# Stick-breaking attention on eight cores: where two pairs of matmuls stand in TensorE's order within a key block

## Chip, cores and metric

The kernel runs on the 8 cores of one Trainium2 chip, each core on its own one of eight sequences, with no exchange between them. The metric is the device time of the slowest core in microseconds, lower is better.

## What is computed

One transformer layer: a layer norm, then attention and a mixture of experts side by side on the normed input, both added to it.

```python
z = einsum('bhid,bhjd->bhij', q, k) / sqrt(64)      # 32 heads of 64, 2048 tokens
mask = tril(ones((l, l)), k=-1)
lom = where(mask, -softplus(z), 0)
s = flip(cumsum(flip(lom, -1), -1), -1) - lom        # sum over the later keys below the query
att = where(mask, exp(log_sigmoid(z) + s), 0)
o = einsum('bhij,bhjd->bhid', att, v)
x = x + (o @ Wo.T) + moe(xn)                         # 32 experts, top 4, low-rank factors, one shared
```

The cumulative sum runs over keys from the last to the first, so key blocks are worked from the diagonal back to key 0 and carry a running sum.

## The kernel before

A small scheduler (`Sched`) records instructions for each engine in the order in which the Python code calls `Sc.op`. That order is each engine's program order, and nothing reorders it later. Waits follow from what an instruction reads and writes: an instruction waits for the last writer of what it reads and for the readers of what it overwrites.

The stages of a core, in time: layer norm and transposes, small projections and the router, attention (from about 829 to 4870 us of the profiled execution), the output projection with `Wo`, and the experts (from about 5.4 ms on).

Attention handles 16 head pairs. For one head pair (`gen_headpair`) the loop runs over 4 query tiles `qt` of 512 queries, and in each over key blocks `jb` of 128 keys, from `4*qt+3` down to 0: 4, 8, 12 and 16 blocks, 40 in all. The first four blocks of a query tile lie on the diagonal: with `c0` = 384, 256, 128 and 0 they work on 128, 256, 384 and 512 query columns for each head, and the mask is added by a further matmul (line 555). The others ("full blocks") have 512 columns and no mask. For each block and both heads of the pair (`hs` = 0, 1):

- scores: `emit_z` writes k times q into the PSUM pair `zpair[jb % 2]` (line 548). There are two such pairs, so scores of block jb-1 overwrite the pair of block jb+1, and have to wait until ScalarE has read that for `att`. The two heads' matmuls stand on different rows of the array, and the trace shows full blocks' pair as one line "x2".
- ScalarE: `texp` = exp(z) (L606, or L614 for each head where c0 > 0), `sp` = ln(1 + texp) (L609 or L618).
- sum: for each head TensorE adds `tri` times sp (L632) and the running sum `lsb` through a one-row matmul (L638) to the scores in PSUM, and forms the block's column sum in `pbL` (L644). VectorE adds that to `lsb` (L649). As there is one `pbL` for both heads, the second head's L644 waits for the first head's L649.
- ScalarE: `att` = exp of the result (L565 or L571).
- output: att times v adds to `pboA` and `pboB` (L579). At the end of a query tile VectorE copies both to `oF` (L658).

The loop is pipelined by hand. `pend` is the block before (jb+1), whose `att` and output are still to come. In the loop body of block jb the order in which instructions are recorded before the change is: texp and sp of jb; `yield`; att and output of jb+1 (`emit_att_o`), scores of jb-1; `yield`; the six sum matmuls of jb with the VectorE adds; `yield`.

At every second `yield` the caller takes one step of `gen_qkv` for the next head pair: 3 steps that issue 16 weight loads each on GpSimd's queue, 12 steps of 16 matmuls of 128x128 by 512 into `pbq` (L510, "projection units" below, followed by a VectorE copy, L516 or L520), and 8 steps with two transposes each (L526, L529). The generator is used up after 48 of the head pair's 124 yields: the projection units lie in query tiles 0 and 1 (yields 8 to 30), the transposes in the end of tile 1 and the start of tile 2 (yields 32 to 46). The rest of tile 2 and all of tile 3 have neither, nor has any tile of the last head pair. At every third yield one of 112 casts of later weights from DRAM to DRAM is issued, also on GpSimd's queue, until they are used up in the third head pair.

Of the kernel before, what the change touches and what calls it, by code (L numbers as in the profile page):

```python
# [204 lines left out]
def build_program(upto="full", taps=()):  # L205
# [13 lines left out]
    def res(name):  # L219
        if name not in R_:  # L220
            R_[name] = Res(name)
        return R_[name]
# [312 lines left out]
    def gen_headpair(hp):  # L535
# [21 lines left out]
                    start=False, stop=True, skip_group_check=True),  # L557
                    reads=[res("idb"), res("mneg")], writes=[pr[pz]])

        def emit_att_o(pjb, qt, jbmax):  # L560
            zp = pjb % 2
            c0 = 128 * max(pjb - 4 * qt, 0)
            first = (pjb == jbmax)
            if c0 == 0:
                Sc.op("ACT", lambda sc, zp=zp: sc.activation(  # L565
                    t_att[zp][:], zpair_ap[zp][:], AF.Exp),
                    reads=[pr[(0 if zp == 0 else 6)], pr[(0 if zp == 0 else 6) + 1]],
                    writes=[res(f"att{zp}")])
            else:
                for hs in range(2):  # L570
                    Sc.op("ACT", lambda sc, zp=zp, hs=hs, c0=c0: sc.activation(  # L571
                        t_att[zp][:, 512 * hs + c0:512 * hs + 512],
                        zpair_ap[zp][:, 512 * hs + c0:512 * hs + 512], AF.Exp),
                        reads=[pr[(0 if zp == 0 else 6) + hs]], writes=[res(f"att{zp}")])
            oc0 = 0 if first else c0
            for hs in range(2):
                po = PO_BANK[hs]
                p0 = 64 * hs
                Sc.op("PE", lambda t, zp=zp, pjb=pjb, p0=p0, oc0=oc0, first=first, po=po, hs=hs: t.matmul(  # L579
                    pbank[po][0:64, oc0:QT],  # L580
                    t_vtok[:, pjb * 128 + p0: pjb * 128 + p0 + 64],
                    t_att[zp][:, 512 * hs + oc0:512 * hs + 512],
                    start=first, stop=True, skip_group_check=not first),
                    reads=[rvtok, res(f"att{zp}")], writes=[pr[po]])

        for qt in range(NQT):
            jbmax = 4 * qt + 3
# [11 lines left out]
            pend = None  # L599
            for jb in range(jbmax, -1, -1):  # L600
                zp = jb % 2
                zres = zpair_res[zp]
                Dd = jb - 4 * qt
                c0 = 128 * max(Dd, 0)
# [16 lines left out]
                            reads=[res(f"texp{zp}")], writes=[res(f"sp{zp}")])  # L621
                yield
                if pend is not None:
                    emit_att_o(pend, qt, jbmax)
                if jb > 0:
                    emit_z(jb - 1, qt, 0)
                    emit_z(jb - 1, qt, 1)
                yield
                for hs in range(2):
                    pz = (0 if zp == 0 else 6) + hs  # L630
                    h0 = 512 * hs
                    Sc.op("PE", lambda t, zp=zp, h0=h0, c0=c0, pz=pz: t.matmul(  # L632
                        zpair_ap[zp][:, h0 + c0:h0 + QT], t_tri[:],
                        t_sp[zp][:, h0 + c0:h0 + QT],
                        start=False, stop=True, skip_group_check=True),
                        reads=[res("tri"), res(f"sp{zp}")], writes=[pr[pz]])
                    if jb != jbmax:
                        Sc.op("PE", lambda t, zp=zp, h0=h0, c0=c0, pz=pz, hs=hs: t.matmul(  # L638
                            zpair_ap[zp][:, h0 + c0:h0 + QT], t_ones1[:],
                            t_lsb[hs][:, c0:QT],  # L640
                            start=False, stop=True, skip_group_check=True),
                            reads=[res("ones1"), res(f"lsb{hs}")], writes=[pr[pz]])
                    if jb != 0:
                        Sc.op("PE", lambda t, zp=zp, h0=h0, c0=c0: t.matmul(  # L644
                            pbank[2][0:1, c0:QT], t_negones[:],
                            t_sp[zp][:, h0 + c0:h0 + QT],
                            start=True, stop=True),
                            reads=[res("negones"), res(f"sp{zp}")], writes=[pr[2]])
                        Sc.op("DVE", lambda v, hs=hs, c0=c0: v.tensor_tensor(  # L649
                            t_lsb[hs][:, c0:QT], t_lsb[hs][:, c0:QT], pbank[2][0:1, c0:QT], op=ALU.add),  # L650
                            reads=[pr[2], res(f"lsb{hs}")], writes=[res(f"lsb{hs}")])
                yield
                pend = jb
            emit_att_o(pend, qt, jbmax)
            for hs in range(2):
                po = PO_BANK[hs]
                p0 = 64 * hs
# [315 lines left out]
```

How the kernel before makes its waits and increments, by code:

```python
                def body(e, ops=ops):  # L151
                    for waits, fn, inc_key, inc_n in ops:
                        for (s, v) in waits:
                            e.wait_ge(handles[s], v)
                        if fn is not None:
                            inst = fn(e)
                            if inc_n:
                                inst.then_inc(handles[inc_key], inc_n)
```

## Time and profile before

| | us |
|---|---|
| median of 3 runs | 8427.57 (8363.21 to 8457.3) |
| the profiled execution | 8471.23 |
| its span, slowest core (core 6) | 8469.7 |
| spans of the other cores | 8333.5 to 8442.5 |

| engine, core 6 | busy, share of the span |
|---|---|
| TensorE matmul | 71% |
| ScalarE | 34% |
| VectorE | 32% |
| GpSimd | 10% |

The mean granted TensorE clock of the cores is 0.711 to 0.726 of full speed. The page's chain that ended last gives TensorE 49% of the span, DMA 17%, VectorE 11% and ScalarE 10%. A share over the whole span is a mean over stages with different limits; the change touches the attention stage alone, so that is where the rows below are from. In the timelines a matmul's duration runs past the start of the next one, because they are pipelined; the spacing of starts is what a matmul costs in a row of them. All rows are of core 6.

### The profile page before, as it was taken

What the parts mean: (1) busy time and instruction counts of PE and PEld (TensorE: products, weight loads), DVE (VectorE), ACT (ScalarE), POOL (GpSimd) and SP (SyncE); (2) the same over time, 40 slices, a digit from 0 to 9 for tenths busy, and PEclk for the clock granted to TensorE, in tenths of its full rate; (3) what the DMA queues carried; (4) which work ended last, traced back from release to release, by engine and by line L of the source; (5) the groups of instructions that cost most, each with busy time, mean ns of one, the idle gap of its engine ahead of it and who ended that gap; (6) DMA issues with size and microseconds to landing.
All of it is one profiled execution on the core that took longest, in us unless ns stands there. A gap on an engine that the chain in (4) does not pass through costs nothing.

```text
span 8469.7 us, 79587 instructions; the slowest of 8 cores (8333.5 to 8469.7 us)
## 1 busy us (share of the span) xinstructions
PE 5973.4 (71%) x18740; PEld 1687.8 (20%) x18740; DVE 2682.5 (32%) x4660; ACT 2880.7 (34%) x4306; POOL 854.0 (10%) x1617
## 2 busy tenths in 40 slices
PE   2223667788888888888888856377767757766775
PEld 0011211122222222222222122122212121122212
DVE  7211212222222222222222201166146416523550
ACT  0000334344444444444444500154034305412440
POOL 0101120111000111100000010100110010011001
PEclk9866665666665566666656579688877788777788
DMA  2001646510000000000000034211421151133115
GB/s 76 12 4 11 74 51 76 66 12 7 7 6 6 7 8 8 8 6 6 6 6 1 1 86 95 67 52 55 142 92 47 57 173 51 62 100 119 55 39 171
DMA packets 222099, 408.71 MB, mean 48 GB/s; under 512 B 141576, under 2 KB 144032, under 8 KB 215760
## 3 DMA queue, kind: packets, MB, share of 16 engines
q0 software_dynamic: 200592, 353.00, 19.5%
q1 hardware_dynamic: 20784, 50.47, 2.4%
q8 instruction: 171, 2.80, 0.1%
q14 instruction: 280, 2.29, 0.1%
q10 hardware_dynamic: 272, 0.14, 0.0%
HBM read 451.83 MB, written 85.07 MB: 63 GB/s over the span
## 4 chain that ended last, share of the span: by engine, by line
PE 49%; DMA 17%; DVE 11%; ACT 10%; issue 9%; another core or an unknown queue 2%; DVEq 1%; ACTq 0%; SPq 0%; POOL 0%; POOLq 0%
PE pbq L510 7%; PE zp L632 6%; PE zp L638 6%; DMA cd<-scr_cd 5%; ACT att L565 4%; DMA xp<-x 4%; PE pboA L579 4%; PE zp L548 3%; DVE gu L825 3%; PE pbL L644 3%; PE pboB L579 2%; ACT g L817 2%; PE pbL L814 2%; PE zp L814 2%
## 5 line engine op out<-in xcount | busy, mean ns | idle before, releaser
L649 DVE TENSOR_TENSOR lsb<-lsb,pbL 1x512 bf16<-1x512 bf16 (+3 forms) x1152 | 673.5, 585 | 1820.5 <-PE pbL L644 1803.9
L606 ACT ACTIVATE texp<-zp 128x1024 bf16<-128x1024 f32 x448 | 458.3, 1023 | 984.7 <-PE zp L548 789.5
L632 PE MATMUL zp<-sp,tri 128*128 128x512 bf16 (+3 forms) x1280 | 652.0, 509 | 5.9 <-ACT sp L618 5.9
L565 ACT ACTIVATE att<-zp 128x1024 bf16<-128x1024 f32 x448 | 458.0, 1022 | 575.5 <-PE zp L638 569.8
L638 PE MATMUL zp<-lsb,ones 1*128 1x512 bf16 (+2 forms) x1152 | 610.7, 530 | 0.0
L579 PE MATMUL pboA<-att,vtok 128*64 128x512 bf16 (+2 forms) x640 | 347.0, 542 | 372.5 <-ACT att L565 303.2
L644 PE MATMUL pbL<-sp,negones 128*1 128x512 bf16 (+3 forms) x1152 | 559.4, 486 | 66.7 <-DVE lsb L649 66.1
L825 DVE TENSOR_TENSOR gu<-g,pbL 128x512 bf16<-128x512 bf16 x704 | 484.1, 688 | 201.7 <-PE pboB L811 87.3
L797 ACT ACTIVATE zg<-zp 128x512 bf16<-128x512 f32 x64 | 38.2, 597 | 1482.3 <-PE zp L794 1482.3
L825 DVE TENSOR_TENSOR gu<-g,zp 128x512 bf16<-128x512 bf16 x704 | 484.1, 688 | 176.8 <-PE zp L811 64.7
L817 ACT ACTIVATE g<-zp 128x512 bf16<-128x512 f32 x704 | 420.3, 597 | 291.4 <-PE zp L811 233.3
L817 ACT ACTIVATE g<-pboB 128x512 bf16<-128x512 f32 x704 | 420.3, 597 | 242.9 <-PE pboB L811 179.4
L609 ACT ACTIVATE sp<-texp 128x1024 bf16<-128x1024 bf16 x448 | 473.1, 1056 | 41.8 <-ACT texp L606 0.8
L927 PE MATMUL zp<-cd,zd 128*128 128x512 bf16 x1024 | 305.6, 389 | 230.9 <-DMA cd<-scr_cd 225.9
L548 PE MATMUL zp<-q,k 64*128 64x512 bf16 (+3 forms) x1280 | 433.1, 509 | 0.0
L722 PE MATMUL zp<-wo,oF 128*128 128x512 bf16 x1024 | 269.0, 423 | 188.7 <-DVE op L735 141.0
L579 PE MATMUL pboB<-att,vtok 128*64 128x512 bf16 (+2 forms) x640 | 357.1, 558 | 0.0
L614 ACT ACTIVATE texp<-zp 128x128 bf16<-128x128 f32 (+2 forms) x384 | 146.4, 381 | 616.5 <-PE zp L555 598.7
L497 POOL DMA_DIRECT2D wq<-WqT x256 | 135.2, 528 | 2116.2 <-PE zp L555 1071.8
L814 PE MATMUL pbL<-zu,cgu 128*128 128x512 bf16 x704 | 309.9, 440 | 53.2 <-DVE gu L825 46.8
L814 PE MATMUL zp<-zu,cgu 128*128 128x512 bf16 x704 | 304.5, 433 | 57.6 <-DVE gu L825 52.2
L811 PE MATMUL zp<-zg,cgu 128*128 128x512 bf16 x704 | 316.1, 449 | 0.8 <-ACT g L817 0.8
(187 smaller groups left out, 7007.0 us busy)
## 6 DMA issues: line engine op xcount, KB each, us to landing
cd<-scr_cd POOLq DMA_DIRECT2D x256, 512.0 KB, 4.7
cgu<-scr_cgu POOLq DMA_DIRECT2D x136, 704.0 KB, 4.5
scr_cgu<-CguT POOLq DMA_DIRECT2D x32, 704.0 KB, 74.3
x<-x SPq DMA_DIRECT2D x16, 1024.0 KB, 4.9
scr_cd<-CdT POOLq DMA_DIRECT2D x32, 512.0 KB, 72.9
xp<-x SPq DMA_DIRECT2D x64, 256.0 KB, 5.2
out<-op SPq DMA_DIRECT2D x64, 256.0 KB, 3.8
out<-yst POOLq DMA_DIRECT2D x16, 1024.0 KB, 7.9
```

Source lines behind the costliest of these rows:

```text
L510: Sc.op("PE", lambda t, hc=hc, nt=nt, bk=bk, wsrc=wsrc: t.matmul(pbank[bk][:, 0:QT], wsrc[:, hc * 128:(hc + 1) * 128], t_xnF[:, hc * S + n ...
L548: Sc.op("PE", lambda t, jb=jb, qt=qt, p0=p0, zp=zp, h0=h0, c0=c0: t.matmul(zpair_ap[zp][:, h0 + c0:h0 + QT], t_k[p0:p0 + 64, jb * 128:(jb ...
L565: Sc.op("ACT", lambda sc, zp=zp: sc.activation(t_att[zp][:], zpair_ap[zp][:], AF.Exp), reads=[pr[(0 if zp == 0 else 6)], pr[(0 if zp == 0 ...
L579: Sc.op("PE", lambda t, zp=zp, pjb=pjb, p0=p0, oc0=oc0, first=first, po=po, hs=hs: t.matmul(pbank[po][0:64, oc0:QT], t_vtok[:, pjb * 128 + ...
L609: Sc.op("ACT", lambda sc, zp=zp: sc.activation(t_sp[zp][:], t_texp[zp][:], AF.Ln, bias=1.0), reads=[res(f"texp{zp}")], writes=[res(f"sp{zp ...
L632: Sc.op("PE", lambda t, zp=zp, h0=h0, c0=c0, pz=pz: t.matmul(zpair_ap[zp][:, h0 + c0:h0 + QT], t_tri[:], t_sp[zp][:, h0 + c0:h0 + QT], sta ...
L638: Sc.op("PE", lambda t, zp=zp, h0=h0, c0=c0, pz=pz, hs=hs: t.matmul(zpair_ap[zp][:, h0 + c0:h0 + QT], t_ones1[:], t_lsb[hs][:, c0:QT], sta ...
L644: Sc.op("PE", lambda t, zp=zp, h0=h0, c0=c0: t.matmul(pbank[2][0:1, c0:QT], t_negones[:], t_sp[zp][:, h0 + c0:h0 + QT], start=True, stop=T ...
L649: Sc.op("DVE", lambda v, hs=hs, c0=c0: v.tensor_tensor(t_lsb[hs][:, c0:QT], t_lsb[hs][:, c0:QT], pbank[2][0:1, c0:QT], op=ALU.add), reads= ...
L814: Sc.op("PE", lambda t, c=c, cur=cur, zu=zu: t.matmul(pbank[b2][:, 0:QT], t_cgu[cur][:, I + c * 128: I + (c + 1) * 128], zu[:], start=True ...
L817: Sc.op("ACT", lambda sc, c=c, g=g: sc.activation(g[:, c * QT:(c + 1) * QT], pbank[b1][:, 0:QT], AF.Silu), reads=[pr[b1]], writes=[rg_])
L825: Sc.op("DVE", lambda v, c=c, g=g, gu=gu: v.tensor_tensor(gu[:, c * QT:(c + 1) * QT], g[:, c * QT:(c + 1) * QT], pbank[b2][:, 0:QT], op=AL ...
```

## The change

`emit_att_o` is split into `emit_att` (ScalarE's exp of block jb+1) and `emit_o` (the output matmuls of block jb+1). `emit_att` stays where it was. The scores of block jb-1 and the output matmuls of jb+1 are now recorded after the six sum matmuls of block jb, just ahead of the third `yield`, the scores first. After the loop both parts are called for the last block, as before. No instruction is added or removed, and the order on ScalarE, VectorE, GpSimd and SyncE stays as it was.

```diff
@@ -557,7 +557,7 @@
                     start=False, stop=True, skip_group_check=True),
                     reads=[res("idb"), res("mneg")], writes=[pr[pz]])
 
-        def emit_att_o(pjb, qt, jbmax):
+        def emit_att(pjb, qt, jbmax):
             zp = pjb % 2
             c0 = 128 * max(pjb - 4 * qt, 0)
             first = (pjb == jbmax)
@@ -572,6 +572,11 @@
                         t_att[zp][:, 512 * hs + c0:512 * hs + 512],
                         zpair_ap[zp][:, 512 * hs + c0:512 * hs + 512], AF.Exp),
                         reads=[pr[(0 if zp == 0 else 6) + hs]], writes=[res(f"att{zp}")])
+
+        def emit_o(pjb, qt, jbmax):
+            zp = pjb % 2
+            c0 = 128 * max(pjb - 4 * qt, 0)
+            first = (pjb == jbmax)
             oc0 = 0 if first else c0
             for hs in range(2):
                 po = PO_BANK[hs]
@@ -621,10 +626,7 @@
                             reads=[res(f"texp{zp}")], writes=[res(f"sp{zp}")])
                 yield
                 if pend is not None:
-                    emit_att_o(pend, qt, jbmax)
-                if jb > 0:
-                    emit_z(jb - 1, qt, 0)
-                    emit_z(jb - 1, qt, 1)
+                    emit_att(pend, qt, jbmax)
                 yield
                 for hs in range(2):
                     pz = (0 if zp == 0 else 6) + hs
@@ -649,9 +651,15 @@
                         Sc.op("DVE", lambda v, hs=hs, c0=c0: v.tensor_tensor(
                             t_lsb[hs][:, c0:QT], t_lsb[hs][:, c0:QT], pbank[2][0:1, c0:QT], op=ALU.add),
                             reads=[pr[2], res(f"lsb{hs}")], writes=[res(f"lsb{hs}")])
+                if jb > 0:
+                    emit_z(jb - 1, qt, 0)
+                    emit_z(jb - 1, qt, 1)
+                if pend is not None:
+                    emit_o(pend, qt, jbmax)
                 yield
                 pend = jb
-            emit_att_o(pend, qt, jbmax)
+            emit_att(pend, qt, jbmax)
+            emit_o(pend, qt, jbmax)
             for hs in range(2):
                 po = PO_BANK[hs]
                 p0 = 64 * hs
```

## Rows read from the trace of the kernel before

**Rows 1.** The page: busy by engine; granted TensorE clock in 40 slices.

```profile
PE 5973.4 (71%) x18740; PEld 1687.8 (20%) x18740; DVE 2682.5 (32%) x4660; ACT 2880.7 (34%) x4306; POOL 854.0 (10%) x1617
...
PEclk9866665666665566666656579688877788777788
```

**Rows 2.** Chain of waits, 3125 to 3137 us: shares by engine and line.

```profile
by line: ACT att L565 25.8%; PE zp L638 18.1%; PE zp L632 18.0%; PE pboA L579 15.2%; PE pboB L579 10.7%; PE zp L548 9.0%; PE pbL L644 8.6%; issue 4.5%; ACTq L154 0.3%
```

**Rows 3.** Timeline, full blocks: start us, us, engine, line, out<-in, [idle <-releaser].

```profile
3126.14 0.61 PE L548 MATMUL zp<-q,k 64*128 64x512 bf16 x2
...
3126.68 0.61 PE L632 MATMUL zp<-sp,tri 128*128 128x512 bf16 x1
3126.89 1.02 ACT L606 ACTIVATE texp<-zp 128x1024 bf16<-128x1024 f32 x1 [1.87 <-PE zp L548]
...
3128.01 1.06 ACT L609 ACTIVATE sp<-texp 128x1024 bf16<-128x1024 bf16 x1
...
3128.81 0.60 PE L638 MATMUL zp<-lsb,ones 1*128 1x512 bf16 x1
...
3129.34 0.59 PE L644 MATMUL pbL<-sp,negones 128*1 128x512 bf16 x1
3129.51 1.02 ACT L565 ACTIVATE att<-zp 128x1024 bf16<-128x1024 f32 x1 [0.45 <-PE zp L638]
...
3130.68 0.61 PE L579 MATMUL pboA<-att,vtok 128*64 128x512 bf16 x1 [0.75 <-ACT att L565]
...
3131.64 0.61 PE L548 MATMUL zp<-q,k 64*128 64x512 bf16 x2
```

**Rows 4.** Windows of 5 us: PE, PEld, DVE, ACT, POOL busy; clock; DMA.

```profile
3015.00:3020.00 5.00, 4.93 (x23) 1.93 (x22) 1.33 (x2) 1.40 (x2) 1.06 (x2) 1.00 0.11 12
...
3060.00:3065.00 5.00, 4.33 (x10) 0.85 (x10) 1.35 (x2) 2.60 (x3) 1.05 (x2) 0.50 0.14 16
```

**Rows 5.** Timeline, stretch with projection work, columns as before.

```profile
3012.53 0.39 PE L632 MATMUL zp<-sp,tri 128*128 128x512 bf16 x1
...
3014.48 0.38 PE L644 MATMUL pbL<-sp,negones 128*1 128x512 bf16 x1 [0.29 <-DVE lsb L649]
...
3014.78 3.63 PE L510 MATMUL pbq<-xnF,wv 128*128 128x512 bf16 x16
...
3026.18 0.22 PE L526 MATMUL pbq<-idb,vF 128*128 128x128 bf16 x1 [0.90 <-DVE vtok L529]
```

**Rows 6.** Timeline, first four blocks of query tile 3, columns as before.

```profile
2860.74 0.28 PE L548 MATMUL zp<-q,k 64*128 64x128 bf16 x1
...
2862.94 0.27 PE L632 MATMUL zp<-sp,tri 128*128 128x128 bf16 x1 [0.16 <-ACT sp L618]
...
2864.42 0.26 PE L644 MATMUL pbL<-sp,negones 128*1 128x128 bf16 x1 [0.80 <-DVE lsb L649]
...
2866.20 0.50 PE L548 MATMUL zp<-q,k 64*128 64x384 bf16 x1
...
2868.79 0.52 ACT L618 ACTIVATE sp<-texp 128x384 bf16<-128x384 bf16 x1
...
2870.74 0.60 PE L548 MATMUL zp<-q,k 64*128 64x512 bf16 x1
...
2872.43 1.02 ACT L606 ACTIVATE texp<-zp 128x1024 bf16<-128x1024 f32 x1 [2.37 <-PE zp L555]
...
2876.45 0.61 PE L548 MATMUL zp<-q,k 64*128 64x512 bf16 x2
```

**Rows 7.** Timeline of VectorE: the copies that close tiles 2 and 3.

```profile
2860.49 0.68 DVE L658 CAST oF<-pboA 64x512 bf16<-64x512 f32 x1 [5.12 <-PE pboA L579]
...
2946.72 0.68 DVE L658 CAST oF<-pboA 64x512 bf16<-64x512 f32 x1 [5.12 <-PE pboA L579]
```

**Rows 8.** TensorE's waits, 829 to 1735 us: total us, times, longest.

```profile
PE pbq L510 <- DMA wk<-WkT: 71.4, 3, 25.8
PE pbq L510 <- DMA wv<-WvT: 67.5, 3, 22.8
```

## The prediction

> **What bounds the kernel now.** I started with the page [rows 1]: TensorE is the busiest engine, at 71% of the span, and in the attention stage (slices 5 to 23) it is granted about 0.6 of its clock. Busy does not mean bounding, so next came the chain of waits over two full blocks of query tile 3 [rows 2]. It never passes through `texp` or `sp`: it goes ScalarE's `att` (25.8%), output matmuls L579, scores L548, the sum matmuls L632, L638 and L644, then `att` again.
>
> The timeline shows that loop [rows 3]. Scores start at 3126.14, the six sum matmuls follow from 3126.68, `att` waits for the second L638 (0.45 us idle), runs from 3129.51 for 1.02 us, the output matmuls start at 3130.68, the next scores at 3131.64. So one full block takes 5.50 us. Meanwhile exp and ln of the next block (3126.89 to 3129.07) run beside the sum matmuls, fully hidden. TensorE's only idle time is 0.75 us, its wait for `att`.
>
> The windows show the clock [rows 4]. In the stretch with projection units it is 1.00, the 2.4 GHz level. In full blocks without them it is 0.50, the 1.2 GHz level, though matmuls fill 4.33 of 5 us. At the high level [rows 5] six sum matmuls start within 1.95 us (3012.53 to 3014.48) against 2.66 us at the low one (3126.68 to 3129.34, [rows 3]).
>
> **The change, full blocks.** Only TensorE's order changes. What it removes from the loop: `att` of jb+1 follows `sp` of jb at once on ScalarE, and TensorE has six sum matmuls to do meanwhile, so the 1.02 us and the 0.75 us wait are hidden. The output matmuls, too: they now run under the next exp and ln. What it adds: scores of jb-1 stand behind all six sum matmuls of jb, those need `sp` of jb, and that needs the scores of jb, which came last. So scores, exp, ln and six sum matmuls form one loop, with nothing beside it but the outputs. TensorE now stands at L632 until `sp` is there, and behind that L632 on its queue are only the other sums and the scores, on which ScalarE's next `texp` waits. From [rows 3]:
>
> scores to start of `texp`, 3126.14 to 3126.89: 0.75. `texp` to the end of `sp`, 3126.89 to 3128.01 + 1.06: 2.18. End of `sp` to the first sum matmul: 0.14, the gap that [rows 6] show (`att` to output is the same, 3129.51 + 1.02 to 3130.68: 0.15). First to last sum matmul: 2.66. Last one to the scores behind it: 0.53, the spacing from L638 to L644. Sum **6.26 us against 5.50: +0.76 per full block**. The wait of the second L644 for VectorE does not appear at the low clock. For `att` there are 3.3 us of cover; without it 1 us would come on top. The term I know least is 0.53, and it could hardly be under 0.4 or over 0.65.
>
> **The first four blocks of a tile** [rows 6]. Before, scores to scores from the first to the fifth block take 2876.45 - 2860.74 = 15.71 us. After, each block costs scores to end of ln, 0.14, sum matmuls, one spacing:
> - 128 columns: scores to sum matmul 2.20 (2860.74 to 2862.94), to the last L644 1.48 (it waits for VectorE, still with its memsets), 0.20. 3.88.
> - 256: scores to end of ln about 2.6, between the 2.06 of 128 columns (2.20 less 0.14) and 3.11 of 384 (2866.20 to 2868.79 + 0.52); 0.14; sum matmuls and spacing about 2.0. 4.8.
> - 384: 3.11 + 0.14 + about 2.6. 5.85.
> - 512 with mask: 1.69 (2870.74 to 2872.43) + 2.18 + 0.14 + 2.66 + 0.53 = 7.2.
>
> Sum 21.7: **+6.0 us per tile**. The interpolated pieces may be off by half a microsecond in all.
>
> **The end of a tile.** Before: the copies of tiles 2 and 3 are 86.2 us apart [rows 7]. Less 15.71 and 11 blocks of 5.50 leaves 10.0 from the last scores to the next tile. After: 0.75 + 2.18 + 0.14, four sum matmuls 2.2 (the last block has no L644), `att` with its latencies 1.25, outputs 0.96: 7.5. **-2.5 per tile**. A tile thus changes by 6.0 - 2.5 plus 0.76 for each full block but the first: tile 3 (11 of them) **+11.9**, tile 2 (7) +8.8.
>
> **Tiles 0 and 1 with projection units** [rows 5]. A unit of 16 matmuls takes 3.63 us and keeps TensorE busy while ScalarE does its 3.3 us. Both orders put units at the same yields: before, some stand ahead of the outputs and some ahead of the sums; after, all lie between outputs and sums, just where the new gap would be, and every block of tile 1 up to the transposes has one or two. Tile 0 has none in its first two blocks, but its first unit starts no later: after, 3.88 + 4.8 + 1.3 (scores) + 0.96 (outputs) = 11.0 us into the tile; before, 10.0 (2860.74 to 2870.74) + about 1.5 for those scores. From there TensorE works without gaps either way, so I take no gain and no loss, except that one set of scores and outputs (about 1.3 us) slips behind the first unit of tile 0, and one out of cover at the end of tile 1: +1.3 each, bounds 0 and 3. The transposes take about 1.3 us per step (a wait of 0.90 for VectorE and two of 0.22); they too fall into the new gap, but two steps share one and stick out. The order on the other engines, GpSimd's queue of loads among them, is the same, so nothing is moved past anything there. Tile 2: +0.5, bounds 0 and 1.6, so +9.3.
>
> **Sum per head pair:** 1.3 + 1.3 + 9.3 + 11.9 = 23.8.
>
> **Head pairs 0 to 2** are another matter. There TensorE waits 71.4 + 67.5 us for weights [rows 8], one wait for `wk` and one for `wv` in each pair, 46 us together, because on GpSimd's queue the loads of the next pair stand behind some 40 casts; that chain runs on its own. Head pairs 1 and 2 have these waits in tiles 0 and 1, and 46 us is more than the 23.8 by which they start late. So what pairs 0 and 1 lose is swallowed there; only tiles 2 and 3 of pair 2 count: +21.2. If nothing is swallowed, it is 48 us more. Pairs 3 to 14: 12 x 23.8 = 286. Pair 15 has no units at all: 11.9 + 8.8 + 5.8 (3 x 0.76 + 3.5) + 2.7 for tile 0 (one masked full-width block, no others) = 29.2. **Sum 286 + 21 + 29 = +336 us.** The other stages keep their code and only start later. Against the profiled execution's own 8471.2 that is 8807; it was 43.7 us above the median of its three runs, so on the median, 8427.6 + 336 = **8764 us**, 4.0% slower.
>
> **The rivals.**
>
> *The clock rises (faster).* TensorE's idle time per full block grows from 0.75 to about 1.5 us and it does the same work, so nothing in the rows hints at the 2.4 GHz level: it is not granted in the denser order [rows 4]. If it were, a full block would take 0.54 + 2.18 + 0.14 + 1.95 + 0.30 = 5.1 us, 0.39 under before; the first four blocks some +3 instead of +6, the end of a tile -4. About -9 us per head pair over 13 of them, and -14 for the last: -130, **8298 us**. It decides from about 72% of those stretches at the high level (336 of 336 + 130); up to about there the loss only shrinks. Chance 4%.
>
> The Trainium skill ("TensorE: Matmul & The Clock Gate", section "Why this matters for your kernels") ties the full clock to keeping TensorE continuously busy, with no long idle gaps. By that rule both orders would have the full clock in full blocks, and the result would be that rival's 8298. The trace does not agree for the order before: 0.50 with 4.33 of 5 us busy.
>
> *The clock is mixed, or the gaps cancel (no change).* At about 70% high clock both effects balance: **8428**. For it speaks only that the projection units keep 1.00. Chance 4%.
>
> *The projection units lose the clock (much slower).* If the new gaps kept it at 1.2 GHz there, each unit would take up to twice its 3.63 us: some 11 units x 3.6 x 13 pairs = 515 on top, **about 9280**. Against it: TensorE has no gap in these stretches. Chance 4%.
>
> *The diagonal blocks are cheaper than I read (less slow).* If the sums of these blocks cost no more than before, 30 tiles lose 6 us less each, 180 in all: **8584**. Against it stand their four separate exp and ln, now all in the loop. Chance 6%.
>
> **How the numbers follow.** Forecast 82%, the four rivals 18%. Its bounds: +-0.12 us on 255 full blocks (+-31), +-0.5 on 30 tiles (+-15), projection tiles -31 to +41, swallowed time 0 to +48, and the runs' own scatter (-64 to +30): together about -80 to +90, so 8685 to 8855, which holds 8 in 10; the rivals lie outside. A difference of 1% (84 us) is about what a measurement of this kernel tells from none. Slower by over 1%: forecast, third and fourth rival, 92%. Within 1%: 4%. Faster: 4%.
>
> **What would show it.** After: full blocks of tile 3 6.2 to 6.3 us apart at a granted clock of 0.50; `att` directly behind `sp` with no wait for L638; `texp` idle over 2.5 us before each block, waiting for the scores L548; L632 waiting for `sp`, which it does almost nowhere now; the chain of waits through `texp` and `sp` instead of `att` and L579; the copies of tiles 2 and 3 98 us apart instead of 86.2; weight waits in pairs 0 to 2 shorter by about 45 us; the same 65 us or so of full clock in each later head pair. I am wrong if the clock row says 1.00 in full blocks, if the spacing is not set by this loop, or if the projection stretches grow.

## The result, and the profile after

The changed kernel takes 8760.4 us (median of 10 runs, 8721.4 to 8805.0) against 8446.6 us for the kernel before on the same chips (10 runs, 8363.2 to 8484.6): a ratio of 1.039, 95% interval 1.035 to 1.043. The forecast was 8764 us, 336 us above the 8427.6 us of the kernel before that it started from; against its own 8446.6 us the changed kernel is 314 us slower. Its profiled execution took 8763.2 us, with a span of 8761.6 us on core 6; that is 292 us more than the span of the profiled execution before.

The page of the changed kernel: busy time by engine, granted clock in 40 slices, and the chain that ended last by engine.

```profile
PE 5957.2 (68%) x18740; PEld 1696.5 (19%) x18740; DVE 2683.2 (31%) x4660; ACT 2844.6 (32%) x4306; POOL 857.7 (10%) x1617
...
PEclk9866666566665666656666557778788888888888
...
PE 47%; DMA 15%; ACT 15%; DVE 11%; issue 10%; DVEq 1%; ACTq 0%; SPq 0%; POOL 0%; POOLq 0%
```

TensorE's busy time hardly moves (5973 to 5957 us) while its share falls from 71% to 68% [rows 1]: it does the same work with more gaps. In the chain ScalarE has gone from 10% to 15%.

The chain of waits over two blocks, by line, after:

```profile
by line: ACT texp L611 25.8%; PE zp L634 18.8%; PE zp L640 17.8%; ACT sp L614 17.8%; PE pbL L646 17.2%; PE zp L548 9.8%; issue 4.7%; ACTq L154 0.6%
```

Before, it went through `att` and L579 and never through `texp` or `sp` [rows 2]. Now `att` and the outputs (L584) are absent, and `texp` (L611) and `sp` (L614) hold 44%. The two loops have changed places.

The timeline of two full blocks after, with the same columns as [rows 3]:

```profile
3301.55 0.59 PE L634 MATMUL zp<-sp,tri 128*128 128x512 bf16 x1 [1.85 <-ACT sp L614]
...
3304.20 0.59 PE L646 MATMUL pbL<-sp,negones 128*1 128x512 bf16 x1
...
3304.72 0.61 PE L548 MATMUL zp<-q,k 64*128 64x512 bf16 x2
...
3305.48 1.02 ACT L611 ACTIVATE texp<-zp 128x1024 bf16<-128x1024 f32 x1 [3.11 <-PE zp L548]
...
3306.59 1.06 ACT L614 ACTIVATE sp<-texp 128x1024 bf16<-128x1024 bf16 x1
3307.55 1.00 ACT L565 ACTIVATE att<-zp 128x1024 bf16<-128x1024 f32 x1
...
3307.79 0.59 PE L634 MATMUL zp<-sp,tri 128*128 128x512 bf16 x1 [1.69 <-ACT sp L614]
```

Sum matmuls start at 3301.55 and, a block later, at 3307.79: 6.24 us. Within it: 2.65 from the first to the last sum matmul, 0.52 to the scores, 0.76 to `texp`, 2.17 to the end of `sp`, 0.14 to the next sum matmul. TensorE stands still for 1.69 us before L634, waiting for `sp`; `att` follows `sp` at once, with no wait.

A window of 5 us after, in full blocks, columns as in [rows 4]:

```profile
3300.00:3305.00 5.00, 3.45 (x8) 0.67 (x8) 0.78 (x2) 2.19 (x4) 0.00 (x0) 0.50 0.00 0
```

The clock of the full blocks is 0.50 as before, with matmuls in 3.45 us of 5 instead of 4.33.

ScalarE's waits from 2000 to 4000 us (us in total, times, longest):

```profile
ACT texp L611 <- PE zp L548: 635.2, 174, 10.9
...
ACT att L565 <- PE zp L640: 56.1, 30, 2.9
```

Over the same window of the kernel before, `texp` waited 408.3 us for scores and `att` 259.7 us for L638. The waits of `att` fall by 204 us, and those of `texp` grow by 227.

The copies that close tiles 2 and 3, after, and TensorE's waits for weights in the first head pairs:

```profile
4373.28 0.68 DVE L666 CAST oF<-pboA 64x512 bf16<-64x512 f32 x1 [6.40 <-PE pboA L584]
...
4471.19 0.68 DVE L666 CAST oF<-pboA 64x512 bf16<-64x512 f32 x1 [6.40 <-PE pboA L584]
```

```profile
PE pbq L510 <- DMA wv<-WvT: 73.1, 3, 25.4
PE pbq L510 <- DMA wk<-WkT: 32.4, 2, 22.2
```

The copies are 97.9 us apart (86.2 in [rows 7]). These waits for weights fall from 138.9 us [rows 8] to 105.5. With the waits for `wq`, which the rows leave out, they fall from 152.6 to 109.4 us; the forecast said about 45 us less.

Where the time went, from the starts of the closing copies (L658 before, L666 after), in us. The pairs are numbered from 0, and the first three columns are of core 6; the fourth is the difference of the medians over the eight cores:

| part | before | after | change | change, median of the cores | forecast |
|---|---|---|---|---|---|
| pair 12, tile 0 | 29.2 | 28.8 | -0.4 | +0.6 | +1.3 |
| pair 12, tile 1 | 62.0 | 64.8 | +2.8 | +3.1 | +1.3 |
| pair 12, tile 2 | 67.1 | 76.0 | +8.9 | +8.9 | +9.3 |
| pair 12, tile 3 | 86.5 | 97.9 | +11.4 | +11.3 | +11.9 |
| pair 15, four tiles | 213.1 | 241.1 | +28.0 | +27.9 | +29.2 |
| pairs 3 to 14 | 2928 | 3246 | +318 | +289 | +286 |
| pairs 0 to 2 | | | +35 | +23 | +21 |
| up to the last copy, sum | | | +381 | +337 | +336 |
| behind the last copy | 3602 | 3513 | -89 | +2 | 0 |

(In the column of the medians, pairs 0 to 2 and the sum count from the first closing copy, on core 6 from the start of the program.)

The last two lines of the table need care. On core 6 the attention stage lost 45 us more than forecast and the stages behind it, whose code is the same, were 89 us shorter. The second is not the change's doing: that core had a mean granted clock of 0.794 there in the execution before and 0.815 after, and the other cores took 3462 to 3568 us before and 3483 to 3537 after, with medians over all eight of 3501 and 3503. The median over the eight cores of the stretch from first to last closing copy is 4003.5 us before and 4340.8 after, +337, beside a forecast of +336. Core 6 is the outlier after: the other cores took 3213 to 3229 us for pairs 3 to 14, against its 3246.

### The profile page after: what moved, and what is told of

It is laid out like the page before. It is cut to its first block, busy times and chain, and to the rows that moved or that the text cites. A ratio compares the mean times of both kernels' runs of the same rounds, so it can differ in the third digit from the quotient of the medians.

```text
span 8761.6 us, 79148 instructions; the slowest of 8 cores (8689.6 to 8761.6 us)
## 1 busy us (share of the span) xinstructions
PE 5957.2 (68%) x18740; PEld 1696.5 (19%) x18740; DVE 2683.2 (31%) x4660; ACT 2844.6 (32%) x4306; POOL 857.7 (10%) x1617
## 4 chain that ended last, share of the span: by engine, by line
PE 47%; DMA 15%; ACT 15%; DVE 11%; issue 10%; DVEq 1%; ACTq 0%; SPq 0%; POOL 0%; POOLq 0%
PE pbq L510 7%; PE zp L634 6%; PE zp L640 6%; PE pbL L646 5%; DMA cd<-scr_cd 5%; ACT sp L614 5%; ACT texp L611 4%; PE zp L548 4%; DVE gu L833 3%; DMA xp<-x 3%; ACT g L825 2%; PE pbL L822 2%; DMA wv<-WvT 2%; PE zp L822 2%; PE zp L819 1%
## 5 line engine op out<-in xcount | busy, mean ns | idle before, releaser
L634 PE MATMUL zp<-sp,tri 128*128 128x512 bf16 (+3 forms) x1280 | 641.2, 501 | 691.1 <-ACT sp L614 567.1
L611 ACT ACTIVATE texp<-zp 128x1024 bf16<-128x1024 f32 x448 | 458.9, 1024 | 1761.0 <-PE zp L548 1447.4
L646 PE MATMUL pbL<-sp,negones 128*1 128x512 bf16 (+3 forms) x1152 | 560.7, 487 | 71.0 <-DVE lsb L651 70.4
L614 ACT ACTIVATE sp<-texp 128x1024 bf16<-128x1024 bf16 x448 | 473.6, 1057 | 41.1
L634 PEld LDWEIGHTS zp<-sp,tri 128*128 128x128 bf16 x1280 | 131.5, 103 | 1240.1 <-issue 1218.3
L584 PE MATMUL pboA<-att,vtok 128*64 128x512 bf16 (+2 forms) x640 | 361.2, 564 | 13.6 <-ACT att L565 13.6
L730 PE MATMUL zp<-wo,oF 128*128 128x512 bf16 x1024 | 292.8, 454 | 111.1 <-DVE op L743 55.8
L584 PE MATMUL pboB<-att,vtok 128*64 128x512 bf16 (+2 forms) x640 | 360.3, 563 | 0.0
```

What stands on the lines that cost most here:

```text
L611: Sc.op("ACT", lambda sc, zp=zp: sc.activation(t_texp[zp][:], zpair_ap[zp][:], AF.Exp), reads=[zres[0], zres[1]], writes=[res(f"texp{zp}")])
L614: Sc.op("ACT", lambda sc, zp=zp: sc.activation(t_sp[zp][:], t_texp[zp][:], AF.Ln, bias=1.0), reads=[res(f"texp{zp}")], writes=[res(f"sp{zp ...
L634: Sc.op("PE", lambda t, zp=zp, h0=h0, c0=c0, pz=pz: t.matmul(zpair_ap[zp][:, h0 + c0:h0 + QT], t_tri[:], t_sp[zp][:, h0 + c0:h0 + QT], sta ...
L646: Sc.op("PE", lambda t, zp=zp, h0=h0, c0=c0: t.matmul(pbank[2][0:1, c0:QT], t_negones[:], t_sp[zp][:, h0 + c0:h0 + QT], start=True, stop=T ...
```

## The experiments

**1. Only the outputs late.** The scores go back ahead of the sums, the outputs stay behind them.

```diff
                 if pend is not None:
                     emit_att(pend, qt, jbmax)
+                if jb > 0:
+                    emit_z(jb - 1, qt, 0)
+                    emit_z(jb - 1, qt, 1)
                 yield
...
-                if jb > 0:
-                    emit_z(jb - 1, qt, 0)
-                    emit_z(jb - 1, qt, 1)
                 if pend is not None:
                     emit_o(pend, qt, jbmax)
```

> Only the output matmuls (L579's place) move behind the sum matmuls; the scores of jb-1 stay ahead of them, as in the kernel before. Loop theory (the time of a block is the longest loop of dependent work): the outputs leave the loop att, scores, sums, att, which becomes 5.50 - 0.96 = 4.54 us, and then TensorE's own work is longer, scores 0.54, six sum matmuls 3.2, outputs 0.96, in all about 4.75 us. Full blocks of query tile 3 4.75 us apart instead of 5.50, tile 3 about 11 us shorter than before (86.2 to about 75), some 20 us per head pair, 8447 to about 8165, ratio 0.967. Rival (the outputs lay beside other work anyway, and only the place of the scores matters): block 5.50 us, ratio 1.00. A further rival: with no gap left on TensorE the clock is granted in full and the block falls below 4.7 us; then the ratio is under 0.95.

Measured: 8131.7 us, ratio 0.965 (0.958 to 0.972). It was run again beside a later variant:

> The first experiment's kernel again, unchanged, beside the one above on the same chip: 8130 us, ratio 0.965, to compare the two.

8161.2 us, ratio 0.966 (0.961 to 0.971). Chain of waits by line, one block of the timeline, and a window of full blocks:

```profile
by line: PE zp L637 27.1%; PE zp L643 21.4%; PE pbL L649 20.7%; PE zp L548 16.2%; PE pboA L584 11.3%; PE pboB L584 8.5%
```

```profile
3421.70 0.61 PE L548 MATMUL zp<-q,k 64*128 64x512 bf16 x2
...
3423.57 1.06 ACT L614 ACTIVATE sp<-texp 128x1024 bf16<-128x1024 bf16 x1
...
3425.08 1.02 ACT L565 ACTIVATE att<-zp 128x1024 bf16<-128x1024 f32 x1 [0.45 <-PE zp L643]
...
3425.43 0.64 PE L584 MATMUL pboA<-att,vtok 128*64 128x512 bf16 x1
...
3426.42 0.61 PE L548 MATMUL zp<-q,k 64*128 64x512 bf16 x2
```

```profile
3420.00:3425.00 5.00, 5.00 (x12) 0.93 (x11) 1.35 (x2) 3.10 (x3) 1.06 (x2) 0.50 0.14 13
```

Scores to scores 4.72 us (expected 4.75). The chain is TensorE alone. Since `att` (3425.08 to 3426.10) has TensorE's outputs of the block before beside it, nothing waits for it, and TensorE is busy in 5.00 us of 5. The loop theory holds, its rival (outputs hidden anyway) and the further rival both fall: the clock stays at 0.50 though the engine has no gap left. The same ratio shows what the change had in it: one of its two moves gains 3.4%.

**2. Only the scores late.**

```diff
                 if pend is not None:
                     emit_att(pend, qt, jbmax)
+                    emit_o(pend, qt, jbmax)
                 yield
...
-                if pend is not None:
-                    emit_o(pend, qt, jbmax)
                 yield
```

> The other half alone: the outputs stay directly behind att and ahead of the sums, the scores of jb-1 move behind the six sums. Loop theory: scores, texp, sp, att, outputs, sums all lie in one loop: 0.75 + 2.18 + 1.08 + 0.96 + 2.66 + 0.53 = 8.2 us per full block of tile 3 (6.26 in the changed kernel, 5.50 before), tile 3 about 125 us long, total about 9400 us, ratio about 1.115. Rival (the loss comes from the place of the outputs): block 5.50 us or less and a ratio of at most 1.00.

One run of 9503 us, against 8450 for the kernel before on the same chip, a ratio of 1.125; full blocks 8.14 us apart (starts of `texp`), tile 3 125.0 us. The chain over two blocks:

```profile
by line: PE zp L635 16.6%; PE zp L641 16.5%; PE pbL L647 15.9%; ACT att L565 14.2%; PE pboA L584 9.3%; PE zp L548 8.7%; ACT sp L614 8.1%; ACT texp L611 8.0%; PE pboB L584 6.6%; issue 3.2%; ACTq L154 0.3%
```

Everything is in the loop now: `texp`, `sp`, `att`, outputs, sums and scores in turn. So the loss belongs to the place of the scores, and late outputs repay part of it. In full blocks, against the 5.50 us before: late outputs alone -0.78, late scores alone +2.64, both +0.74 us. The two moves do not add up, since a loop is the longest path and not a sum of parts.

**3 and 4. How many sum matmuls stand ahead of the scores.** Three, with the scores between the two heads:

```diff
                             reads=[pr[2], res(f"lsb{hs}")], writes=[res(f"lsb{hs}")])
-                if jb > 0:
-                    emit_z(jb - 1, qt, 0)
-                    emit_z(jb - 1, qt, 1)
+                    if hs == 0 and jb > 0:
+                        emit_z(jb - 1, qt, 0)
+                        emit_z(jb - 1, qt, 1)
```

> The changed kernel with the scores of jb-1 placed behind the three sum matmuls of the first head, ahead of the second head's three; outputs last. Loop theory: three spacings of 0.53 leave the loop of 6.26: 4.67 us, and TensorE's own work of about 4.75 us per block is longer. Blocks of tile 3 4.75 us apart, tile 3 about 10 us shorter than before (about 76.5), total about 8190, ratio 0.970. Rival (it is not the six sums in the loop, but having scores behind sums at all): block 6.2 us, ratio 1.04 as in the changed kernel.

8174 us, ratio 0.966 (0.960 to 0.973). Two starts of `texp` in tile 3:

```profile
3312.93 1.02 ACT L611 ACTIVATE texp<-zp 128x1024 bf16<-128x1024 f32 x1 [1.64 <-PE zp L548]
...
3317.65 1.02 ACT L611 ACTIVATE texp<-zp 128x1024 bf16<-128x1024 f32 x1 [1.63 <-PE zp L548]
```

4.72 us, with matmuls in 5.00 us of 5 from 3312 to 3317 and from 3317 to 3322: TensorE's own work again. Scores behind sums are no loss in themselves; six sums ahead of them are.

Four, with both L646 behind the scores (`if jb != 0:` and its two instructions go into a second loop over the heads behind `emit_z`):

> The changed kernel with the scores behind L634 and L640 of both heads (four matmuls) and ahead of both L646; outputs last. Loop theory: two spacings of 0.53 less than 6.26: 5.20 us per full block of tile 3, that tile about 84 us, total about that of before, ratio 0.99 to 1.01. Together with the run with three this gives the slope: 0.53 us for each matmul ahead of the scores, down to the 4.75 us of TensorE's own work. Rival (a fixed cost of the scores waiting for att, not for the matmuls ahead of them): the same 6.2 us as in the changed kernel.

5.71 us per block and not 5.20, tile 3 88.6 us and not 84, one run of 8564 us, 1.013 of the kernel before and not 0.99 to 1.01. The expectation missed by 0.5 us, and the timeline says where:

```profile
3435.10 0.61 PE L548 MATMUL zp<-q,k 64*128 64x512 bf16 x2
...
3435.64 0.59 PE L651 MATMUL pbL<-sp,negones 128*1 128x512 bf16 x1
...
3436.33 0.68 DVE L656 TENSOR_TENSOR lsb<-lsb,pbL 1x512 bf16<-1x512 bf16 x1 [3.52 <-PE pbL L651]
3436.97 1.06 ACT L614 ACTIVATE sp<-texp 128x1024 bf16<-128x1024 bf16 x1
...
3437.16 0.58 PE L651 MATMUL pbL<-sp,negones 128*1 128x512 bf16 x1 [0.93 <-DVE lsb L656]
...
3438.66 0.61 PE L634 MATMUL zp<-sp,tri 128*128 128x512 bf16 x1
...
3440.81 0.61 PE L548 MATMUL zp<-q,k 64*128 64x512 bf16 x2
```

Scores 3435.10, first column sum at 3435.64, VectorE's add until 3437.01, second column sum at 3437.16, the outputs behind it, and the next sum matmul only at 3438.66. `sp` was ready at 3438.03, and 0.14 later TensorE could have begun: it came 0.49 us late. The one `pbL` for both heads had entered the loop. That was a guess until the next run.

**5. The outputs between the two column sums.**

```diff
+                for hs in range(2):
+                    h0 = 512 * hs
+                    if hs == 1 and pend is not None:
+                        emit_o(pend, qt, jbmax)
                     if jb != 0:
```

> The run with four matmuls ahead of the scores gave 5.71 us per block and not 5.20. Theory: there the two L646 stand next to each other, the second waits for VectorE's add (0.7 + 0.68 + 0.14 us), and with the outputs behind it TensorE reaches the next sums only 0.56 us after sp is ready. Here the outputs stand between the two L646 and fill that wait: 5.20 us per block of tile 3, total about 8430. Rival (a fixed cost of scores behind sums, about 0.5 us): 5.71 as before.

```profile
3155.62 1.02 ACT L611 ACTIVATE texp<-zp 128x1024 bf16<-128x1024 f32 x1 [2.11 <-PE zp L548]
...
3160.81 1.02 ACT L611 ACTIVATE texp<-zp 128x1024 bf16<-128x1024 f32 x1 [2.11 <-PE zp L548]
```

5.19 us (expected 5.20), tile 3 82.2 us. The total, one run of 8350 us, is 80 us under the expected 8430; from the first to the last closing copy the median of the cores is 3969 us against 4003.5 before, and the rest of the difference lies outside the attention stage and was not followed up. The slope is as the theory says: with six sum matmuls ahead of the scores 6.24 us, with four 5.19, 0.53 each, and with three 4.72, where the theory's 4.67 meets TensorE's own work.

**6. The wait of two units in a row.** Tile 1 grew by 2.8 us where 1.3 was forecast. TensorE's waits in one head pair of the changed kernel, 4200 to 4470 us:

```profile
PE pbq L510 <- DVE k L516: 1.9, 2, 0.9
PE pbq L510 <- DVE vF L516: 1.3, 1, 1.3
```

They are three, of about 1 us each, and the kernel before has one of 0.2 in a head pair. At three places in tile 1 the third yield of one block and the second of the next both bring a projection unit. Before, scores and sums or outputs stood between them; after, nothing does, and the second unit's first matmul waits until VectorE has copied `pbq`. The experiment puts the third yield ahead of the scores:

```diff
+                yield
                 if jb > 0:
                     emit_z(jb - 1, qt, 0)
                     emit_z(jb - 1, qt, 1)
                 if pend is not None:
                     emit_o(pend, qt, jbmax)
-                yield
```

> The changed kernel with its third yield ahead of the scores and outputs, so that two projection units never follow each other directly. Theory of the single bank (two units in a row share pbq, and the first L510 of the second waits 0.9 us for VectorE's copy, three such places in tile 1): those waits are gone, tile 1 of the later head pairs falls from about 65 to about 62.5 us where the clock is granted in full; full blocks of tile 3 stay at 6.24 us and tiles 2 and 3 at 76 and 98. Rival (tile 1 grew for lack of cover for texp and sp): moving a unit ahead of the scores takes cover away, tile 1 grows beyond 65.

The waits in one head pair of it:

```profile
PE pbq L510 <- DVE k L516: 0.2, 1, 0.2
```

Tile 1 takes 62.8 to 63.8 us where the clock is granted in full (64.6 to 65.9 in the changed kernel), tile 3 97.6 to 97.9, full blocks 6.23. So the waits are worth about 2 us per head pair. About 1.3 us against before remain, as much as the forecast put there; what they consist of was not looked into. The total, one run of 8769 us, does not resolve 25 us.

**7 and 8. Without the casts.** Both kernels with the casts taken out of the attention loop; the code behind it issues them.

```diff
-            if scast_thunks and step % 3 == 0:
-                scast_thunks.pop(0)()
```

> The kernel before, with the 112 casts of later weights issued after the attention stage and not within it; nothing else is changed, and the total is longer, since the output projection then waits for casts. Only the time from the first to the last closing copy (L658) counts, 4003 us in the kernel before. The theory that casts delay the weight loads of head pairs 0 to 2: those waits are gone, all head pairs take 244.5 us, the stretch is about 3855 us.

> The changed kernel with the casts issued after the attention stage. Compared with the kernel before without casts, over the same stretch. If the waits for weights swallowed part of the loss, the difference grows from the 340 us that most cores show with casts to about 390 us, some 4245 us in all, as every head pair now pays its 24 to 26 us. If nothing was swallowed it stays at 340.

| us | with casts, before | after | without casts, before | after |
|---|---|---|---|---|
| pairs 1 and 2 together, slowest core | 595.7 | 597.6 | 488.0 | 533.0 |
| first to last closing copy, median of the cores | 4003.5 | 4340.8 | 3933.1 | 4273.5 |

Pairs 1 and 2 show it plainly: with casts the change costs them 1.9 us, without casts 45.0, twice 22.5. The weight loads of the first head pairs swallow what the change adds. The whole stretch does not show it as expected: 3933 instead of 3855, and a difference of 340, not 390. Two things were wrong there. Pair 0's tile 1 takes 110 us without casts too, with waits of 23.2 and 21.8 us for weights, so these do not come from the casts; and in the run of the kernel before five later head pairs had 66 to 71 us in tile 1 instead of 62, at a granted clock of 0.81, some 40 us in all, which the changed kernel's run had not. It was so on all cores: pairs 3 to 14 took 2958 to 2978 us in that run, against 2927 to 2939 in the kernel before with casts. Taking these out leaves a difference of about 380, but this correction is argued, from one run each. The expected longer total did not come either: 8330 us without casts against 8421 with them, one run each, and the stages behind the last copy took 3470 to 3523 us, against 3462 to 3602 with them. (The changed kernel without casts took 8634 us.)

**9. The best order, one step further.** Experiment 1 with the outputs ahead of the second L646:

```diff
+                    if hs == 1 and pend is not None:
+                        emit_o(pend, qt, jbmax)
                     if jb != 0:
                         Sc.op("PE", lambda t, zp=zp, h0=h0, c0=c0: t.matmul(
                             pbank[2][0:1, c0:QT], t_negones[:],
...
-                if pend is not None:
-                    emit_o(pend, qt, jbmax)
                 yield
```

> The kernel with early scores and late outputs (first experiment), its outputs now ahead of the second head's L646 instead of behind it. At the low clock nothing waits there, so full blocks of tile 3 stay at 4.72 us, TensorE's own work. At the high clock the second L646 waits about 0.3 us for VectorE in each block with projection units, and the outputs now fill that: some 11 blocks x 0.3 = 3 us per head pair, tile 1 from 61 to about 58.5, about 40 us in all, 8130 to about 8090, ratio 0.958 to 0.962. Rival (TensorE does not get ahead there, since it is VectorE's chain that bounds): no change, ratio 0.965.

8135 us, ratio 0.963 (0.957 to 0.968), beside 0.966 (0.961 to 0.971) for experiment 1 on the same chip: the totals don't tell them apart. TensorE's waits from 1800 to 4500 us, first this kernel's, then those of experiment 1:

```profile
PE pbL L651 <- DVE lsb L656: 28.8, 49, 1.2
```

```profile
PE pbL L649 <- DVE lsb L654: 53.6, 137, 1.2
```

The wait for VectorE falls to about half (from 137 times to 49), tile 1 of pairs 4 to 14 goes from 61.0 to 59.8 us (median), and full blocks stay at 4.72. The mechanism is there, at half the size expected. Part of what is filled in one place is waited for at another: TensorE's waits at the transposes (L526) grow from 63.8 to 74.2 us in the same stretch.

**10 and 11. The clock.** In all kernels so far the full blocks ran at 0.50. Here the small sum matmuls are made full size, in number and result the same: the running sum's row is padded with 127 rows of zeros, and the column sum is taken as one column of a product with `tri`, whose first column is all -1.

```diff
-    t_lsb = [sb(f"lsb{i}", [1, QT], BF16, s2) for i in range(2)]
+    t_lsb = [sb(f"lsb{i}", [128, QT], BF16, s2) for i in range(2)]
+    t_onesw = sb("onesw", [128, 128], BF16, s2)
...
-                            zpair_ap[zp][:, h0 + c0:h0 + QT], t_ones1[:],
+                            zpair_ap[zp][:, h0 + c0:h0 + QT], t_onesw[:],
...
-                            pbank[2][0:1, c0:QT], t_negones[:],
+                            pbank[2][:, c0:QT], t_tri[:],
```

First in the changed kernel's order:

> The changed kernel with its two small kinds of sum matmul made full size, at the same number and with the same result: the running sum's matmul (1 row) now runs over 128 rows, of which 127 are zero, and the column sum's (1 column) over 128 columns, of which one is used. Order and everything else stay. This puts the rival of the rising clock to the test. If the granted clock of the full blocks rises from 0.50 to 1.00, the loop is 0.54 + 2.18 + 0.14 + 1.95 + 0.30 = 5.1 us instead of 6.24, the total about 8300 or less, ratio under 0.98. If it stays at 0.50, the loop can lose only the part of the 0.53 spacing that is not the 512 columns (0.43 at 1.2 GHz), so 5.7 to 6.24 us and a ratio of 1.01 to 1.04. A result of 5.1 at 0.50 would speak against the loop theory.

8464 us (median of 10 runs, 8419 to 8548), ratio 1.005 (1.000 to 1.011), between the two outcomes that the expectation gave. Windows of tile 2, columns as in [rows 4]:

```profile
3325.00:3330.00 5.00, 4.12 (x13) 1.38 (x13) 0.97 (x4) 2.44 (x7) 1.06 (x2) 0.50 0.16 16
3350.00:3355.00 5.00, 3.11 (x9) 0.64 (x7) 1.35 (x2) 2.21 (x4) 1.05 (x2) 0.77 0.15 15
3355.00:3360.00 5.00, 3.81 (x10) 0.85 (x10) 1.35 (x2) 2.63 (x3) 0.72 (x2) 0.66 0.14 13
3360.00:3365.00 5.00, 2.49 (x10) 0.75 (x10) 1.35 (x2) 3.10 (x4) 0.86 (x2) 1.00 0.14 13
```

The clock goes up and down: 0.50 in the tile's first blocks, then 0.66 to 1.00 in these windows of its full ones. Its mean over tile 3 is 0.59 to 0.71 in head pairs 3 to 15. The timeline shows the sum matmuls at both levels:

```profile
3338.84 0.63 PE L644 MATMUL zp<-lsb,onesw 128*128 128x512 bf16 x1
...
3339.27 0.63 PE L650 MATMUL pbL<-sp,tri 128*128 128x512 bf16 x1
...
3344.42 0.38 PE L638 MATMUL zp<-sp,tri 128*128 128x512 bf16 x1 [1.94 <-ACT sp L618]
...
3344.63 0.38 PE L644 MATMUL zp<-lsb,onesw 128*128 128x512 bf16 x1
```

Their starts are 0.43 us apart at the low level and 0.21 at the high one. The same places in the kernels with small sum matmuls have 0.53 and 0.32. So with equal shapes in a row each step is 0.1 us shorter at either level, on top of what the clock gives. Full blocks take 4.9 us where it is high all along (the expectation said 5.1) and 5.3 to 6.0 else, tile 3 85 to 91 us. This is the forecast's second rival, the mixed clock that cancels the loss, brought about by another edit: the block's loop is what it was, only its matmuls start closer together and run faster.

Then in the order of experiment 9:

> The best order so far (early scores, outputs ahead of the second head's column sum) with the same full-size sum matmuls. At 0.50 its blocks are bound by TensorE's own work, 4.72 us; with spacings of 0.43 to 0.53 that is 4.2 to 4.7 and a ratio of 0.93 to 0.96. If the granted clock of the full blocks is 1.00, TensorE has only about 2.8 us of work and ScalarE's loop (exp, ln, exp, and the wait for the scores between them, 3.2 + 0.7) bounds: 3.9 us per block, total about 7850 to 7900, ratio about 0.935.

7741.7 us, ratio 0.917 (0.910 to 0.924), the fastest of all. Windows of full blocks in tile 2, and ScalarE's timeline there:

```profile
3385.00:3390.00 5.00, 2.90 (x13) 1.00 (x14) 1.63 (x3) 3.64 (x4) 0.69 (x3) 1.00 0.14 13
3395.00:3400.00 5.00, 3.20 (x13) 0.86 (x11) 1.97 (x4) 4.24 (x5) 0.53 (x1) 1.00 0.08 8
```

```profile
3397.58 1.02 ACT L615 ACTIVATE texp<-zp 128x1024 bf16<-128x1024 f32 x1 [0.67 <-PE zp L552]
3398.69 1.06 ACT L618 ACTIVATE sp<-texp 128x1024 bf16<-128x1024 bf16 x1
3399.65 1.00 ACT L569 ACTIVATE att<-zp 128x1024 bf16<-128x1024 f32 x1
3401.33 1.02 ACT L615 ACTIVATE texp<-zp 128x1024 bf16<-128x1024 f32 x1 [0.67 <-PE zp L552]
```

The clock is 1.00, and a block takes 3.75 us (expected 3.9), tile 3 60 us. `texp`, `sp` and `att` follow each other, with 0.67 us until the next scores: the scores overwrite the PSUM pair that `att` reads, and start 0.14 us after `att` ends (3400.80). ScalarE's loop is the bound now, and TensorE has matmuls in about 3 of 5 us only. The total came out over 100 us under the 7850 to 7900 of the expectation. That expectation prices the full blocks alone; but tile 3 is about 14.4 us shorter than in experiment 9, of which the full blocks explain about 11, and tile 1 is about 3 us shorter. How much of the gain is the clock and how much the closer starts was not separated. By an estimate, closer starts alone could take at most six times 0.1 us from the 4.72, down to 4.1, so the step to 3.75 needs the clock. Nor was it tested whether the one-row matmul or the one-column matmul, made full size alone, would raise it.

## Why the prediction was right

- **The loop of a full block** was the term that carried the sum: 6.26 us forecast, 6.24 measured, at the clock of 0.50 that was taken from the row. Its parts: sum matmuls 2.66 and 2.65, the least known spacing 0.53 and 0.52, `texp` and `sp` 2.18 and 2.17, latency 0.14 and 0.14, scores to `texp` 0.75 and 0.76. Experiments 1 to 5 show that it is a loop and which of TensorE's instructions lie on it; that `texp` and `sp` do is read from the chain of waits.
- **The first four blocks**: 3.88, 4.8, 5.85 and 7.2 forecast; from scores to scores pair 12's tile 3 takes 3.88, 4.69, 5.79 and 7.16 us. The end of that tile, forecast 7.5, takes about 7.7. Tiles 2 and 3 are within 0.5 us of their forecast, and pair 15, which has no units, within 1.2 of 29.2.
- **Tile 1 was mis-sized**: 1.3 forecast, 2.8 measured in pair 12 of core 6, 3.2 in the mean over pairs 3 to 14 (median of the cores). The step "all lie between outputs and sums, just where the new gap would be ... I take no gain and no loss" looked at the gap and not at `pbq`: units that moved together now share one PSUM bank with nothing in between. About 2 us per head pair, shown by experiment 6.
- **Tile 0** was forecast 1.3 longer and is 0.4 shorter in pair 12; over pairs 3 to 14 it is 0.3 longer (median of the cores). So a head pair's 24 us come out right in part by luck: tile 1 costs 2 us more than forecast, tiles 0, 2 and 3 together about as much less.
- **Pairs 0 to 2**: +21 forecast, +35 on core 6, +23 by the medians over the cores. The account holds: what tiles 2 and 3 of pair 0 lose (+20.4 us on core 6) comes back in tiles 0 and 1 of pair 1 (-19.4), what those of pair 1 lose (+20.6) in pair 2 (-19.8), and tiles 2 and 3 of pair 2 count in full (+20.5). Core 6 has 12.6 us on top in pair 0's tile 1 and ahead of its first closing copy, which the forecast put at nothing; 5.5 us of that lie before attention begins, where the code is the same. One reason given was wrong for pair 0: its waits for weights do not come from the casts (experiment 7).
- **The clock rivals** did not occur. The 0.50 of the full blocks held; in the projection units core 6 was granted 0.81 and not 1.00 for a part of the time in four head pairs (tile 1 68 to 75 us there, about 25 us in all). As the kernel before shows the same in another run (experiment 7), it is no effect of the change that these runs could separate.
- **The median** of 8764 against 8760 is closer than the parts deserve: +381 and -89 us on the profiled core, of which the second goes with the clock behind the attention stage. The base was off too: the kernel before had 8427.6 us in the three runs that the forecast started from and 8446.6 us in ten, and the difference of the totals is 314 us, not 336. That 8764 and 8760 agree to 4 us is luck. The medians over the cores, +337 against +336, are the fairer comparison for the attention stage.

## What to carry to other kernels

Before moving an instruction later in an engine's order, write down the loop from one block's first result to the next one's and add its pieces from the timeline: what leaves the loop is gained only until the next longest loop, or the engine's own work, bounds, and what enters it is paid in full. Here late outputs alone gave -3.4%, late scores alone +12.5%, both +3.9%. Look at a shared buffer too when two pieces of work come to stand side by side, and read the granted clock of the very stretch: making small matmuls larger without changing their number took another 4.8% off the best order (8135 to 7742 us), more than the 3.7% that reordering had taken off the kernel before.

## What the runs showed of the hardware

- TensorE's granted clock did not follow its busy time. With one-row and one-column matmuls among the sums it was 0.50 in full blocks at 3.45, 4.33 and 5.00 us of 5 busy (changed, before, experiment 1); with the same number of full-size matmuls it was 1.00 at about 3 of 5 (experiment 11), and went up and down in experiment 10. That the edit raised it is shown; what in it did, and why, is not. The Trainium skill ("TensorE: Matmul & The Clock Gate", section "Why this matters for your kernels") advises to keep TensorE busy without long gaps for the full clock; experiment 1 has no gap and did not get it.
- Matmuls of equal shape in a row start closer together. The step from one sum matmul to the next is 0.53 us at the low and 0.32 us at the high level where one-row, one-column and full-size matmuls alternate, and 0.43 and 0.21 us where all are full size (experiment 10). The traces show a difference in the weight loads, which take about 0.10 us. Between unequal shapes a load starts only with its own matmul (at 3127.21 for the matmul at 3127.22, kernel before); between equal ones it starts with the matmul before (at 3344.42 for the matmul at 3344.63, experiment 10). A load that is no longer hidden would fit the 0.1 us, but was not tested by itself, and any other cost of changing shape would fit as well:

```profile
3127.21 0.10 PEld L638 LDWEIGHTS zp<-lsb,ones 1*128 1x128 bf16 x1 [0.44 <-issue]
```

```profile
3344.42 0.10 PEld L644 LDWEIGHTS zp<-lsb,onesw 128*128 128x128 bf16 x1
```

- There is a third level of the granted clock, and it differs between cores of one execution and between executions of one kernel. In the profiled execution before, four cores had none of it and the others 160 to 540 us; in the changed kernel it was 416 to 922 us, and in the same kernel without casts none. A window of tile 1 of the changed kernel, first core 6, then core 0 at the same time (columns as in [rows 4]):

```profile
3945.00:3950.00 5.00, 5.00 (x19) 1.74 (x18) 0.69 (x1) 2.00 (x4) 0.00 (x0) 0.81 0.00 0
```

```profile
3945.00:3950.00 5.00, 4.05 (x20) 1.69 (x18) 0.69 (x1) 1.66 (x5) 1.05 (x2) 1.00 0.10 11
```
